# The far masks of key tiles 12 to 29: a GpSimd comparison in place of a ScalarE activation

## The reference, cut to what matters

```
src, dst = (edge_index[0], edge_index[1])
alpha = leaky_relu(oi @ q + kj @ k)              # one number for each edge
m = segment_max(alpha, dst, num_segments=n_nodes)
e = exp(alpha - m[dst])
z = segment_sum(e, dst, num_segments=n_nodes)
```

## Time and profile before

| | us |
|---|---|
| median of three runs | 3185.24 |
| profiled execution, its own time | 3187.04 |
| profiled execution, span of the core | 3185.3 |
| VectorE busy in the span | 2038.5 (64%) |
| ScalarE busy | 1246.7 (39%) |
| GpSimd busy | 291.8 (9%) |
| the phase that is changed: `cnt` of k = 12 to `cnt` of k = 29 | 137.54 to 227.29, that is 89.75 |

### The profile page before, as it was taken

The page is one execution under the profiler, slowest core; times in us unless marked ns, Lnnn a source line. Parts: engine busy times, 40 slices in busy tenths (PEclk is TensorE's granted clock), DMA queues, the critical chain, the costliest instruction groups (busy, mean ns, idle before and its releaser), DMA issues. The chain is left out here.

```text
span 3185.3 us, 34821 instructions
## 1 busy us (share of the span) xinstructions
PE 2715.0 (85%) x12628; PEld 2009.0 (63%) x12629; DVE 2038.5 (64%) x2828; ACT 1246.7 (39%) x1496; POOL 291.8 (9%) x146
## 2 busy tenths in 40 slices
PE   7877965888666974997999996997999899999979
PEld 3556962333236972554999995996888655566654
DVE  6765997999853545990888885803676872114451
ACT  1563217888510001111777782224655620004310
POOL 0000000000025852000000001510000000000020
PEclk9998557999867997999999997998999989998979
DMA  1566426111026535533665542625333611000031
GB/s 65 142 178 172 161 87 259 33 49 49 2 82 208 202 132 188 200 103 106 187 172 147 137 112 92 201 77 159 119 126 96 206 33 60 30 0 31 1 88 49
DMA packets 155535, 361.22 MB, mean 113 GB/s; under 512 B 27289, under 2 KB 77921, under 8 KB 154627
## 3 DMA queue, kind: packets, MB, share of 16 engines
q1 hardware_dynamic: 110460, 269.89, 27.8%
q10 hardware_dynamic: 35968, 73.97, 6.5%
q0 software_dynamic: 8960, 15.41, 1.9%
HBM read 276.26 MB, written 82.91 MB: 113 GB/s over the span
## 5 line engine op out<-in xcount | busy, mean ns | idle before, releaser
L1295 PE MATMUL rg1a_acc<-rg1a_values,rg1a_high 125*125 125x193 f32 x2400 | 402.0, 332 | 36.3 <-DVE rg1a_high L1370 34.7
L1295 PEld LDWEIGHTS rg1a_acc<-rg1a_values,rg1a_high 125*125 125x125 f32 x2400 | 400.0, 191 | 38.6 <-issue 36.1
L1497 PE MATMUL gat_acc<-far_u,gat_ft 125*65 125x512 f32 x720 | 288.0, 541 | 72.2 <-DVE far_u L1560 71.8
L1497 PEld LDWEIGHTS gat_acc<-far_u,gat_ft 125*65 125x65 f32 x720 | 94.4, 142 | 262.1 <-issue 171.7
L1359 DVE TENSOR_TENSOR rg1a_high<-rg1a_high,rg1a_lowb 125x1250 f32<-125x1250 f32 x120 | 175.1, 1459 | 120.9 <-ACT rg1a_lowb L1319 120.8
L1096 PE MATMUL rg_out<-rg_w,rg_hT 128*125 128x384 f32 x720 | 234.3, 489 | 0.0
L2012 PE MATMUL rg2a_acc<-rg2a_value_part,rg2a_wts_part 125*125 125x512 f32 x600 | 206.3, 344 | 28.9 <-DVE rg2a_wts_part L1736 19.4
L2013 PE MATMUL rg2a_acc<-rg2a_value_part,rg2a_wts_part 125*125 125x512 f32 x600 | 206.8, 345 | 0.0
L2014 PE MATMUL rg2a_acc<-rg2a_value_part,rg2a_wts_part 125*125 125x512 f32 x600 | 205.2, 342 | 0.0
L1096 PEld LDWEIGHTS rg_out<-rg_w,rg_hT 128*125 128x125 f32 x720 | 135.8, 189 | 97.4 <-issue 1.5
L1318 ACT ACTIVATE rg1a_high<-rg1a_rows,rg_ks 125x1250 f32<-125x1250 f32 x120 | 160.5, 1337 | 84.1 <-PE rg1a_acc L1295 66.8
(11 more groups left out here) (433 smaller groups left out, 5158.1 us busy)
## 6 DMA issues: line engine op xcount, KB each, us to landing
rg2a_values<-values_dram SPq DMA_DIRECT2D x90, 384.0 KB, 3.1
rg1a_counts<-counts_dram SPq DMA_DIRECT2D x40, 820.3 KB
rg_mask<-far_dram SPq DMA_DIRECT2D x60, 312.5 KB, 3.3
moe_raw<-in_L_ffn_w SPq DMA_DIRECT2D x16, 1152.0 KB, 5.7
gat_rows<-rows_dram SPq DMA_DIRECT2D x12, 1250.0 KB, 5.7
rg1a_rows<-shift_dram SPq DMA_DIRECT2D x12, 1250.0 KB, 10.4
relw_chunk<-in_L_gnn_W ACTq DMA_DIRECT2D x36, 384.0 KB, 3.1
sorted_dram<-gat_zeros SPq DMA_DIRECT2D x30, 384.0 KB, 11.0
```

The costliest lines, as they stand in the source:

```text
L1295: last = pe.matmul(tile_of(h, d), wts[i % HB][:, d * TP:(d + 1) * TP], stream[i % VB][:, :], start=first and d % 2 == 0, stop=final, skip_ ...
L1497: last = pe.matmul(acc[h % 2][0:WIDTH, b, 0:c1 - c0], ft[:, t, h, :], wts[i % HB][:, c0:c1], start=(t == 0), stop=(t == NT - 1))
```

## The change

From key tile 12 on (`LATE = 12`), GpSimd makes the far mask with `tensor_scalar`: `(cnt == 0) * 1e30` (`FAR` is -1e30), input float32, output bfloat16, 125 x 1250: the same values. It waits for the copy of this key tile (`sums_copied`) and for the transfer that last read the `far` buffer. ScalarE leaves these 18 masks out. It gets one new wait: before it overwrites `cnt[k % 2]` for k = 14 and later, the mask of k - 2 must be done.

```diff
+        LATE = 12
@@ gpsimd
+            for k in range(LATE, KT):
+                pool.wait_ge(sums_copied, k + 1)
+                pool.wait_ge(far_out[k % 2], k // 2 * 32)
+                pool.tensor_scalar(far[k % 2][:, :], cnt[k % 2][:, :], 0.0, -FAR, op0=ALU.is_equal,
+                                   op1=ALU.mult).then_inc(far_done, 1)
@@ scalar
             def make_far(k):
+                if k >= LATE:
+                    return
                 if k >= 2:
                     act.wait_ge(far_out[k % 2], k // 2 * 32)
                 act.activation(far[k % 2][:, :], cnt[k % 2][:, :], ACT.Relu, bias=far_value[:, 0:1],
                                scale=FAR).then_inc(far_done, 1)
@@
                 act.wait_ge(sums_done, k + 1)
+                if k >= LATE + 2:
+                    act.wait_ge(far_done, k - 1)
                 act.activation(cnt[k % 2][:, :], sums_flat[k % 2][:, 0:N], ACT.Copy).then_inc(sums_copied, 1)
```

## The result

The changed kernel takes 3253.21 us (median of six runs, 3250.56 to 3305.96) against 3187.51 for the kernel before (six runs). The ratio is 1.0208, with a 95% interval of 1.0187 to 1.0228: 2.1% slower, where 0.2% slower was forecast. The run of 3305.96 us, which has the lowest granted clock of the six (0.879 against 0.895 to 0.899), is left out of the ratio. The profiled spans are 3248.8 and 3185.3 us, 63.5 apart.

The account below looks back on a forecast made before the run. VectorE (88% busy) and ScalarE (82%) were taken as nearly full in the four-hot stretch. Four-hot +4.8, six-hot +3.2 and phase end -0.5 gave +7.5 us on 3185.24: 3192.7 us, range 3179 to 3212 (8 in 10).

Parts of the forecast that it names:

- D: Duration of one GpSimd mask instruction in the late key tiles; taken as 1.77 us, though no row showed it.
- the sum: VectorE's work plus holds per period, less the present length, with the phase's end: 4.8 + 3.2 - 0.5 = +7.5 us.
- The hold: GpSimd's mask blocks VectorE's hots in the late key tiles, the two taking turns by instruction: 1.65 us per mask.
- The rule D - 0.12: Hold H on VectorE's hots equals the mask's duration less about 0.12 us, giving 1.65 us.
- the four-hot periods: Twelve copy-to-copy periods, VectorE making four hots for the next key tile; 58.43 us, hold added in full, +4.8 us.
- the six-hot ones: Five copy-to-copy periods with six hots, 31.32 us; VectorE's idle time takes up part of the hold, +3.2 us.
- the fourth rival: TensorE's clock falls behind longer gaps in every four-hot tile, about 1 us more each: +19.5 us, 3204.7; chance 0.08.
- The first rival: GpSimd's comparison in the late tiles is short, holding VectorE 1.05 us: -2.5 us, 3182.7; chance 0.28.
- the second: GpSimd's mask is as long as a two-operand addition, holding VectorE 2.8 us: +28 us, 3213; chance 0.18.
- No hold: GpSimd's masks leave VectorE's hots alone, so earlier masks and less ScalarE work decide: -7.6 us, 3177.6; chance 0.10.
- the early masks and ScalarE's relief: Late tiles: merges stop waiting for mask loads, 3.3 + 0.84 us; ScalarE gains 3.0, phase end 0.5.
- The new waits: ScalarE's wait for the mask of k - 2 before its copy, and GpSimd's own waits: no cost.

Follow-up runs that it names:

- run 5: Kernel before, ScalarE still making all masks, plus the same GpSimd comparison and product into a spare tile nobody reads; 3243.8 us.
- run 8: Changed kernel with GpSimd's mask as minimum with 1 and product, in place of comparison and product; 3248.78 us.
- run 1: Changed kernel with GpSimd's mask as product and sum in place of comparison and product; 3184.28 us.
- run 2: Changed kernel with GpSimd's mask as the comparison alone, without the product; 3225.88 us.
- run 12: Changed kernel with GpSimd's mask as one product, no second operation; 3223.28 us.
- run 15: Changed kernel with GpSimd's mask as sum and product in one instruction of 1250 columns; 3192.95 us.
- run 3: Changed kernel with GpSimd writing only 2 of each mask's 1250 columns, all transfers kept; 3179.79 us, ratio 0.9969 to the kernel before.
- run 4: Kernel before, with ScalarE making each mask directly behind its copy, ahead of counts groups 0 and 1; 3182.08 us, ratio 0.9983.
- run 6: Kernel before, plus a GpSimd memset of 5200 columns into a spare tile at each late key tile; 3250.09 us.

## Why the prediction was wrong
**The term that failed is D, the duration of GpSimd's mask.** The prediction bounded it by 1.18 us (a write-only row) and 2.9 us (a two-operand addition, scaled) and took 1.77. It is 4.43 undisturbed and 4.60 in the mean (run of the changed kernel, runs 5 and 8). Both bounds were rows of other instructions, and I took the two-operand addition for the worst case since it reads most. What sets the price is the form of the operations: for 1250 columns sum with product 1.24 us; one product or one comparison alone 3.4; comparison or minimum with a product 4.4 (runs 1, 2, 8, 12, 15). "GPSIMD Engine Reference" of the Trainium skill, section 4.1, calls one-input work roughly line-rate; the trace agrees for the two sum-product pairs (1.24 us is 1.2 cycles a column, an estimate at the page's 1.2 GHz) and disagrees for the comparison (4.25 cycles). Section 3.1 of that page of the Trainium skill gives 1.8 cycles as the best case, for a tight loop unrolled by four; neither form is near it, and the quick one is below it. (By the prediction's own 1.04 us for the line rate, the sum gives about -4 us, not the -2.5 that it states.)

**The hold was right as a mechanism; its working came out in the total and not in the parts.** The rule D - 0.12 is a little high: 1.24 and 4.43 us held for 1.0 and 4.2. With run 1's mean of 1.44 us, which contains GpSimd's own waits for VectorE, it gives H = 1.3 and the sum 43.4 + 12 x 1.3 - 58.4 = +0.6 for the four-hot periods, 0.65 + 4 x 0.2 = +1.45 for the others and -0.5 at the end, +1.5 us. Measured is 235.41 - 233.97 = +1.4, but from other parts: -2.1 in the four-hot periods, +4.1 in the six-hot ones. So the near hit of the total, in one execution, is partly luck. With 4.3 for the changed kernel the sum gives 36.6 + 16.5 + about 2 = +55 against +59.2 measured, and again the parts are off: the four-hot periods lost 86.59 - 58.43 = 28.2 us, the six-hot ones 60.19 - 31.32 = 28.9. The prediction put one hold into each period; in fact they come in pairs, as at 197.97 and 202.62, and some periods have none (4.09 us) and others two (13.6 us).

**TensorE's clock, the fourth rival**, fell as that rival said: the mean of 0.8 costs 17.9 us of matmul time. Little of it can have been on the path. A slower TensorE would show as idle time of VectorE, and that is 15.6 us between the copies of k = 12 and 29, against 15.9 in run 3 and 11.4 in run 1. So a few microseconds may be the clock's; no run separates them.

**The first rival (short comparison) and the second (long)** differ from what happened in D alone; the long one at 2.9 us was still too short. **No hold** is refuted by the stretched hots and by run 5. What it put on the other side is confirmed: with the hold gone (run 3) the early masks and ScalarE's relief are worth 7.1 us of phase, 7.6 worked out, and run 4 shows that they can be had by order alone. **The new waits cost nothing**, as said: run 3 has them all, and in the changed kernel's trace ScalarE never waits for GpSimd.

**The range** reached only to 3212 since it was built on D's bounds; with an operation that no row shows, its upper end should have stood open.

**What stays open.** Why one instruction of 1250 columns in a slow form holds VectorE through its whole time, and one of 1000 only for 0.77 us at its start and 0.75 at its end. The holds of the short ones grow with the columns, each by 0.5 to 0.8 us a thousand (0.13 us for 250, 0.45 for 625), as if VectorE waited only while the data move in and again while they move out. Run 1's 1250 quick columns (one hold of 1.0 us, with 1.24 us of work) and run 6's memset (4.43 us for 5200 columns, 0.85 a thousand) could be movement of data for the whole of their time; only the 1250 slow columns don't fit. That GpSimd takes in some thousand values ahead would explain it, but no run shows it. Why two operations of sum and product are quicker than one is open too.

## What to carry to other kernels
Before elementwise work is moved to GpSimd beside a busy VectorE, time that very form alone: between two forms of the same shape lay a factor of 3.6. (The quick forms of runs 1 and 15 give wrong masks where a pair has two or more edges, so they are measurements, not a replacement.) Count as its cost what it holds VectorE, and keep each instruction short: 1000 columns and 250 in two instructions held VectorE about a quarter as long (17 us of the phase) as 1250 in one did (64). Even so the phase was longer than in the kernel before with every mask of comparison and product in pieces (norm at 247 to 255 us against 234). First look whether the engine that has the work can do it at another place in its order; in the profiled executions that gave 6.6 us of phase, where the change without its hold gave 7.1, and it needs no second engine.

## What the runs showed of the hardware that I had not expected
- GpSimd's `tensor_scalar`, 1250 columns, float32 to bfloat16: 1.24 us for two of sum and product; 3.38 for one product; 3.37 for one comparison; 4.43 for comparison or minimum with product. Two operations can be quicker than one.
- VectorE is held by a GpSimd instruction that only writes: beside a memset of 5200 columns (4.43 us) a `key_hot` of 0.25 us lasts 4.50 us. The Trainium skill, "SBUF — State Buffer", section "Who interferes with whom", has the port pair that VectorE and GpSimd share held for the whole instruction; the traces agree for 1250 columns of the slow forms (4.2 of 4.43 us) and for the memset, and disagree for 1000 columns and fewer, which hold it at their start and at their end and leave it free between (2 x 0.76 of 3.55 us, 2 x 0.13 of 1.06).
